# Two graph layers on one core: the second layer's denominators move into the pass that computes its scores, and TensorE's counts in the edge passes are raised by drains

## What is computed

```python
# layer one: attention with 8 heads of 32, over the edges of each destination
score = clip(sum(q[dst] * k[src]) / sqrt(32), -10, 10)
alpha = softmax over the edges of one dst
wv = segment_sum(alpha * v[src], dst);  y = wv @ Wp.T + bp;  x1 = x + y
x1 = x1 + gelu(layernorm(x1) @ W1.T + b1) @ W2.T + b2
x = layernorm(x + x1)
# layer two: scores per edge, softmax over the edges of one SOURCE
z = leaky_relu(proj_s[src] + proj_t[dst], 0.2)
e = z @ W_attn.T
e_exp = exp(e - max of e over the edges of src)
denom = segment_sum(e_exp, src)
agg = segment_sum(x[src] * (e_exp / denom[src]), dst)
x = layernorm(x + agg @ W_fc.T + b_fc)
```

## Time and profile before

| what | us |
|---|---|
| median of three runs | 3942.93 |
| lowest and highest of them | 3939.38, 3952.08 |
| span of the profiled execution | 3995.8 |
| PE, PEld busy in it | 2303.1, 1677.2 |
| DVE, ACT, POOL busy in it | 2175.4, 1124.8, 1960.5 |

### The profile page before, as it was taken

How to read it: one execution, slowest core, us unless ns; L and a number is a source line. 1 busy time by engine, 2 the same in 40 slices (tenths; PEclk the granted TensorE clock), 3 DMA queues, 4 the chain that set the end, 5 groups by cost and what they waited for, 6 DMA issues and landing times.

```text
span 3995.8 us, 54572 instructions
## 1 busy us (share of the span) xinstructions
PE 2303.1 (58%) x11454; PEld 1677.2 (42%) x11455; DVE 2175.4 (54%) x6197; ACT 1124.8 (28%) x2699; POOL 1960.5 (49%) x1970
## 2 busy tenths in 40 slices
PE   4456666666666664878233333333334395777776
PEld 2244444444444443756122222222122294656655
DVE  5455655556555564242344444444444596677676
ACT  0144554445544553333111111111112100111111
POOL 0255555555555553121566666666656303544443
PEclk9788877788778877988666666667666656988898
DMA  4666656666666663121677777777767505666564
GB/s 141 195 179 178 182 176 180 175 180 181 177 178 176 176 177 100 50 86 47 191 215 221 212 211 214 211 214 228 210 206 216 175 0 186 205 197 204 183 208 150
DMA packets 365707, 698.62 MB, mean 175 GB/s; under 512 B 77317, under 2 KB 247039, under 8 KB 365674
## 3 DMA queue, kind: packets, MB, share of 16 engines
q0 software_dynamic: 134784, 425.63, 36.1%
q1 hardware_dynamic: 220602, 256.40, 20.6%
q10 hardware_dynamic: 10288, 16.23, 1.1%
HBM read 597.23 MB, written 100.85 MB: 175 GB/s over the span
## 4 chain that ended last, share of the span: by engine, by line
another core or an unknown queue 27%; PE 26%; DVE 24%; issue 16%; DMA 3%; DVEq 2%; SPq 1%; POOL 1%; ACT 1%; ACTq 0%; POOLq 0%
PE ps_px L900 7%; DVE sb_prod L1622 4%; DVE sb_wide L1615 4%; DVE sb_score L1468 4%; PE ps_pa L913 3%; PE ps_px L913 2%; PE ps_px L998 2%; PE ps_px L1007 2%; PE ps_pa L1058 2%; PE ps_pn L1045 2%; DVE sb_wide L1477 1%; PE ps_px L876 1%; DVE sb_parts L1814 1%; DVE sb_prod L1462 1%
## 5 line engine op out<-in xcount | busy, mean ns | idle before, releaser
L900 PE MATMUL ps_px<-sb_parts 128*128 x2430 | 468.2, 358 | 798.8 <-DVE sb_wide L1615 563.1
L900 PEld LDWEIGHTS ps_px<-sb_parts 128*128 128x128 bf16 x2430 | 268.1, 122 | 999.4 <-DVE sb_wide L1615 625.6
L779 POOL DMA_INDIRECT sb_ring<-kv_rows,sb_idx x324 | 322.5, 995 | 357.8 <-DVE sb_wide L1477 152.6
L913 PE MATMUL ps_pa<-sb_wide,sb_onehot 128*128 128x264 f32 x864 | 302.8, 483 | 317.1 <-DVE sb_wide L1477 256.2
L779 POOL DMA_INDIRECT sb_ring<-proj_rows,sb_idx x324 | 316.5, 977 | 303.8 <-issue 170.8
L779 POOL DMA_INDIRECT sb_parts<-kv_rows,sb_idx x324 | 316.0, 975 | 206.9 <-DVE sb_wide L1477 107.4
L1142 ACT ACTIVATE sb_parts<-sb_bits,sb_nn_tab 128x768 bf16<-128x768 int16 x135 | 126.3, 937 | 1016.6 <-remote 606.9
L900 PE MATMUL ps_px<-sb_parts,sb_xwm 128*128 x2430 | 397.9, 309 | 19.2 <-ACT sb_xwm L1147 14.6
L779 POOL DMA_INDIRECT sb_w<-narrow_rows,sb_idx x324 | 315.3, 973 | 163.7 <-issue 102.2
L913 PE MATMUL ps_px<-sb_wide,sb_onehot 128*128 128x264 f32 x756 | 252.9, 466 | 197.3 <-DVE sb_wide L1477 124.3
L779 POOL DMA_INDIRECT sb_w<-feat_rows,sb_idx x162 | 158.9, 981 | 416.0 <-issue 192.3
(11 more groups left out here) (256 smaller groups left out, 4473.2 us busy)
## 6 DMA issues: line engine op xcount, KB each, us to landing
sb_bits<-dst_short SPq DMA_DIRECT2D x280, 192.0 KB
x_edges<-sb_ring SPq DMA_DIRECT2D x54, 768.0 KB
sb_slots<-x_edges SPq DMA_DIRECT2D x54, 768.0 KB
x_edges<-sb_slots SPq DMA_DIRECT2D x27, 768.0 KB
sb_w<-x_edges SPq DMA_DIRECT2D x27, 768.0 KB
sb_msg<-lo_rows SPq DMA_DIRECT2D x28, 576.0 KB
kv_rows<-sb_slots ACTq DMA_DIRECT2D x25, 256.0 KB, 2.8
sb_parts<-part_rows SPq DMA_DIRECT2D x28, 193.5 KB
```

The source lines that it names most:

```text
L779: pool.indirect_dma_start(out=out[:, i, :], out_offset=None, in_=rows, in_offset=bass.IndirectOffsetOnAxis(ap=idx[:, 2 * p + i:2 * p + i + ...
L900: mm = pe.matmul(into, hots_t[L][:, 2 * p + i, :], flat(visit_parts[:, bass.ds(parity, 1), a, 0:width]), start=(a == 0), stop=(a == 2))
L913: mm = pe.matmul(into[:, 0:C + H], onehot[:, j, :], sums_in[:, 2 * (p % FLIGHT) + i, :], start=(p % EARLY == 0 and i == 0), stop=True, ski ...
```

## The change

**Denominators.** They are summed in pass two: the visit v's while pass two is at v + 1. ACT takes the exponentials of the visit's 30 columns, and makes the one-hots of the sources' low bits, 30 rows and 5 Relus, behind the next visit's destination one-hots. DVE does the split and the product in small steps between the pairs 3 to 7; PE does the 30 matmuls in five sets of six behind `expand` of the pairs 10 to 14. As shift it takes the maximum over the first visit, found by a transpose and a matmul on PE during the second. The last visit's share comes after the loop. The slow path gets a sum of its own. `x1` is read in five parts, each waited for by its part of `feats`, and pass three's first one-hots are built ahead of `feats`.

**Counts.** In pass one `expd[0]` and `summed` become one semaphore, `stepped`, raised by a drain once a step, after both `sum_pair(p)` and `expand(p + 9)`. In pass two a drain behind each `expand` raises `expd[1]`, and one behind each set of denominators raises `dpe`. In pass three a drain behind each `sum_rows` raises `slots_free[2]`. A drain is an instruction of its own behind the matmuls, which carries the count in their place.

```diff
@@ expand
-                        mm = pe.matmul(into, hots_t[L][:, 2 * p + i, :], flat(visit_parts[:, bass.ds(parity, 1), a, 0:width]),
-                                       start=(a == 0), stop=(a == 2))
-                mm.then_inc(expd[L], 1)
+                        pe.matmul(into, hots_t[L][:, 2 * p + i, :], flat(visit_parts[:, bass.ds(parity, 1), a, 0:width]),
+                                  start=(a == 0), stop=(a == 2))
+                if L:
+                    pe.drain().then_inc(expd[1], 1)
@@ sum_pair
-                mm.then_inc(summed, 1)
@@ pass one, PE's visits
                         expand(0, C, after, v + 1, p + AHEAD - PAIRS)
+                    pe.drain().then_inc(stepped, 1)
@@ pass two, PE
-            with pe.Fori(0, TD // DT // 2) as it:
-                for b in range(2):
-                    pe.wait_ge(dv, it * 2 + b + 1)
-                    for j in range(DT):
-                        mm = pe.matmul(pn[:, 0:3 * W], lo_hot[:, b, :, j], hi_ex[:, b, :, :, j].rearrange("p a n -> p (a n)"),
-                                       start=False, stop=True, skip_group_check=True)
-                    mm.then_inc(dpe, 1)
+            def denominators(v, g):
+                if g == 0:
+                    pe.wait_ge(dv, v + 1)
+                pe.wait_ge(den_lo, v * HALVES + g + 1)
+                for j in range(g * R, (g + 1) * R):
+                    pe.matmul(pn[:, 0:3 * W], lo_hot[:, j, :], hi_ex[:, :, :, j].rearrange("p a n -> p (a n)"),
+                              start=False, stop=True, skip_group_check=True)
+                pe.drain().then_inc(dpe, 1)
...
+                for p in range(PAIRS):
+                    expand(1, CW, parity, v, p)
+                    if second and p == 2:
+                        top_transposed()
+                    if second and p == 4:
+                        top_spread()
+                    if earlier is not None and p >= PAIRS - HALVES:
+                        denominators(earlier, p - (PAIRS - HALVES))
@@ pass three, sum_rows
-                mm.then_inc(slots_free[2], 1)
+                pe.drain().then_inc(slots_free[2], 1)
@@ ACT, pass two
+            def score_exps(v):
+                act.wait_ge(zs, v * len(ZS) + ZS["masked"])
+                act.wait_ge(shift_set, 3)
+                act.activation(ex_v, dots[:, 2], ACT.Exp, bias=shift[:, 0:1]).then_inc(den_ex, 1)
+
+            def low_sources(v):
+                t0 = visit_value(act, "tile", v)
+                for g in range(HALVES):
+                    act.wait_ge(dpe, v * HALVES + g + 1)
+                    act.sem_inc(act_seen, 1)
+                    for j in range(g * R, (g + 1) * R):
+                        ins = act.activation(lo_hot[:, j, :], iota[:], ACT.Abs, bias=src_lo[:, bass.ds(t0 + j, 1)], scale=-1.0)
+                    ins.then_inc(lo_away, 1)
...
+            node_half(0)
+            with act.Fori(0, total - 1) as u:
+                node_half(act.snap(u + 1))
+                score_exps(u)
+                low_sources(u)
+            low_sources(last_visit(act))
+            score_exps(last_visit(act))
@@ DVE, pass two
+                if step == "high":
+                    t0 = visit_value(dve, "tile", v)
+                    dve.tensor_tensor(hi_hot, iota_j, src_hib[:, bass.ds(t0, G)].unsqueeze(1).broadcast_to([P, W, G]), ALU.is_equal).then_inc(dh, 1)
+                if step == "ex":
+                    dve.wait_ge(den_ex, v + 1)
+                    dve.tensor_tensor(left0, ex_v, kept, ALU.mult).then_inc(dsplit, 1)
...
+                if step == "spread":
+                    done("part2")
+                    dve.wait_ge(dh, v + 1)
+                    dve.wait_ge(dpe, v * HALVES + HALVES)
+                    dve.tensor_tensor(hi_ex, hi_hot.unsqueeze(1).broadcast_to([P, 3, W, G]),
+                                      ex_parts.unsqueeze(2).broadcast_to([P, 3, W, G]), ALU.mult).then_inc(dv, 1)
+
+            WEIGHED = {3: ["ex"], 4: ["part0"], 5: ["left1"], 6: ["part1", "high"], 7: ["left2", "part2", "spread"]}
@@ waits on PE's counts, pass one
-                dve.wait_ge(expd[0], v * PAIRS + p + 1 + PAIRS)
+                dve.wait_ge(stepped, v * PAIRS + p + 1 + PAIRS)
...
-                act.wait_ge(summed, v * PAIRS + p + 1)
+                act.wait_ge(stepped, v * PAIRS + p + 1 + AHEAD + PAIRS - FLIGHT)
@@ SP, after pass two
-            sp.dma_start(x1, proj_rows[:, CW:ROW].rearrange("(w p) c -> p w c", p=P)).then_inc(x1_back, 16)
+            for i in range(NB):
+                some = slice(i * W // NB, (i + 1) * W // NB)
+                sp.dma_start(x1[:, some], proj_rows[i * W // NB * P:(i + 1) * W // NB * P, CW:ROW].rearrange("(w p) c -> p w c", p=P)).then_inc(x1_back[i], 16)
...
-            sp.wait_ge(fv, FVS["recip2"])
             low_rows(tile)
+            features(0)
+            sp.wait_ge(fv, FVS["den0"])
             for c in range(THIRDS):
                 stream(tile, c)
-            features(0)
```

More of the change, by code:

```diff
@@ L289, in build @@
         hot = [sem(f"hot{L}") for L in (0, 1)]
-        expd = [sem(f"expd{L}") for L in range(2)]
+        expd = [None, sem("expd1")]
         dgs = sem("dgs")
@@ new lines, in _, with scored, rows, attend @@
+            WEIGHED = {3: ["ex"], 4: ["part0"], 5: ["left1"], 6: ["part1", "high"], 7: ["left2", "part2", "spread"]}
+            def scored(v, earlier=None, second=False):
+                t0 = visit_value(dve, "tile", v)
+                def rows(p):
+                    dve.wait_ge(expd[1], v * PAIRS + p + 1 + PAIRS)
+                    landed(dve, 1, total, v, p)
+                    dve.tensor_tensor(zbuf[:, pair(p), :], px[:, places(p), 0:CW], proj_slots(p)[:, :, 0:CW], ALU.add).then_inc(slots_free[1], 1)
+                def attend(p):
+                    dve.wait_ge(slots_free[1], v * PAIRS + p + 1 + PAIRS)
+                    dve.tensor_copy(low_dots[:, :, 2 * p:2 * p + 2].rearrange("p c j -> p j c"), zbuf[:, pair(p), C:CW])
+                    for i in (0, 1):
+                        ins = dve.scalar_tensor_tensor(out=prod[:, p % 3, i * C:i * C + C], in0=zbuf[:, 2 * (p % FLIGHT) + i, 0:C], scalar=0.0, in1=attn_hi[:],
+                                                       op0=ALU.max, op1=ALU.mult, accum_out=dots[:, 0, 2 * p + i:2 * p + i + 1])
+                    if p == PAIRS - 1:
+                        ins.then_inc(zs, 1)
+                rows(0)
+                for p in range(PAIRS):
+                    if p + 1 < PAIRS:
+                        rows(p + 1)
+                    attend(p)
+                    if second and p == 0:
+                        dve.wait_ge(shift_pe, 1)
+                        dve.tensor_reduce(top[0:1, 1:2], pa[0:1, 0:P], AX, ALU.max).then_inc(shift_set, 1)
+                    if second and p == 2:
+                        dve.wait_ge(shift_pe, 2)
+                        dve.tensor_scalar(shift[:], pa[:, P:P + 1], -1.0, None, ALU.mult).then_inc(shift_set, 1)
+                    if earlier is not None:
+                        for step in WEIGHED.get(p, []):
+                            weighed(earlier, step)
+                def at(name):
+                    return v * len(ZS) + ZS[name]
+                dve.wait_ge(zs, at("dots"))
+                dve.tensor_tensor(dots[:, 1], dots[:, 0], low_dots[:, 0], ALU.add).then_inc(zs, 1)
+                dve.wait_ge(zs, at("low"))
+                dve.tensor_tensor(dots[:, 2], dots[:, 1], low_dots[:, 1], ALU.mult).then_inc(zs, 1)
+                dve.tensor_copy(kept, low_dots[:, 1]).then_inc(zs, 1)
+                dve.wait_ge(zs, at("kept"))
+                if earlier is None:
+                    dve.tensor_reduce(top[:, 0:1], dots[:, 2], AX, ALU.max).then_inc(shift_set, 1)
+                some = e_all[:, bass.ds(t0, G)]
+                dve.tensor_tensor(some, some, dots[:, 2], ALU.add).then_inc(zs, 1)
+                dve.wait_ge(zs, at("added"))
+                dve.sem_inc(dve_seen, 1)
@@ L1643, in _ @@
+            scored(0)
+            scored(1, 0, second=True)
+            with dve.Fori(0, total - 2) as u:
+                scored(dve.snap(u + 2), dve.snap(u + 1))
             for c in range(THIRDS):
@@ L1645, in _ @@
                 dve.sem_inc(dve_seen, 1)
+            last = last_visit(dve)
+            for step in ("high", "ex", "part0", "left1", "part1", "left2", "part2", "spread"):
+                weighed(last, step)
             dve.memset(e_all[:, T:TPAD], -FAR).then_inc(sv, 1)
@@ L1837, in _ @@
             high_onehots(0)
+            for i in range(NB):
+                some = slice(i * W // NB, (i + 1) * W // NB)
+                dve.wait_ge(x1_back[i], 16)
+                dve.tensor_tensor(feats[:, some, :], x1[:, some, :], denom[:, 2, some].unsqueeze(2).broadcast_to([P, W // NB, C]), ALU.mult).then_inc(fv, 1)
             reciprocals(0)
```

194 lines of the change are left out of this document (107 added, 87 removed).

## The result

The changed kernel took 4121.53 us (median of four runs, 4112.31 to 4139.45) against 3947.51 for the kernel before on the same chip (median of four, the three shown ahead and one more): a ratio of 1.0453, 95% interval 1.042 to 1.0486. It is slower by 4.5%, where 3430 us was forecast. The profiled execution has a span of 4117.1 us, 121.3 more than that of the kernel before, 3995.8.

What follows compares the result with a forecast made beforehand. Bound taken as POOL's gather issue plus waits for late matmul-carried counts. Pass one -265, pass two -122, pass three -12, tail -121 sum to -520: 3995.8 to 3476, scaled to 3430 us; range 3330 to 3560, 8 in 10 3330 to 3870.

Steps and rivals of the forecast that it cites:

- What bounds the kernel: Passes one and two: POOL's gather issue is the floor, 37.7 us a visit; above it, matmul-carried counts arrive 6 to 19 late.
- The old stage, -121: Between last scores and pass three's first gather: moving denominators into pass two saves 121 us, bounds -130 to -108.
- What pass two takes on: Pass two: moved denominator work on DVE, PE and ACT hides under POOL's 37.7 us a visit; 3.3 left for it and other waits.
- The drains, 0.45 where PE is the bound: All three passes: each drain costs 0.45 us where PE is the bound, 0 where it waits anyway; bounds 0.05 and 1.2.
- -554: Whole kernel: sum in us if a drain cost only 0.18 us, pass three's exposed drains costing 24 instead of 60.
- a third, 60 us: Pass three: the share taken of its drains' full 182 us, since PE idles 6.0 of 24.0 us a visit.
- The late counts: All passes: drain counts arrive promptly, so late-count waits go; passes one and two fall to 41 us a visit, pass three -12.
- -265 and -122: Forecast savings in us from passes one and two, each falling to 41 us a visit from 51.2 and 45.7.
- Rival A: All passes: drains wait for late completions and stop PE; at 1.2 us a drain +191, 4130 us scaled; chance 0.15.
- B: All passes: a drain's count is as late as a matmul's, nothing cured; 3883 us scaled; chance 0.08.
- C: Passes one and two: partial cure, pass one falls to 46 us a visit, pass two gains nothing; 3679 us scaled; chance 0.12.
- D: Pass two: DVE's new bf16 steps hold up POOL's issue, at most 2 us a visit, +52 us, inside the forecast's range.

Runs made afterwards that it cites:

- drains_p1: Kernel before with only pass one's two counts merged into one raised by a drain, chip 0: ratio 1.022, pass one 1395.2 us.
- change_third: The changed kernel run again, against the kernel before on chip 12, which has no late counts: ratio 1.0115.
- no_gathers_p1_b: drains_p1 with pass one's gathers after the first visit replaced by POOL writing one column, late chip 11, one run: pass one 873.3 us.
- p3_bare: Kernel before with a drain carrying nothing behind each pass-three sum_rows, count still on the matmul, chip 15: ratio 1.0439, pass three 598.8 us.
- p3_twice: Kernel before with two drains behind each pass-three sum_rows, the second carrying the count, chip 15: ratio 1.0554, pass three 633.7 us.

## Why the prediction was wrong

*What bounds the kernel.* Right in what it saw, as far as it went: POOL's issue is the floor, and on the chips without late counts passes one and two lie on it at 39 us. But the trace was taken for the kernel's own nature. It was also the chip's.

*The old stage, -121.* Right: 133.3 to 13.8 is -119.5, the first gather 4 us sooner, together -124.

*What pass two takes on, nothing beyond a share of 3.3 a visit.* On the chips without late counts 15 us, 0.6 a visit: right. On the late chips 22 to 51 us: 0.9 to 2 a visit, inside the share that was left, but of a gain that did not come.

*The drains, 0.45 where PE is the bound.* Right: 0.45 to 0.55 measured between two groups in a row (1.32 to 1.42 for 0.87), 0.34 in the mean of pass three; the loss of overlap and the restart were both there. The Trainium skill's 175 ns alone (TensorE: Matmul & The Clock Gate, Single matmul latency) would have been too little: the 0.20 of idle comes on top. (The sum that the prediction gives for it, -554, should be -556: 24 for 60 in -520.) The term mis-sized was how many drains bind in pass three. I took a third, 60 us, for PE's idle 6.0 us a visit; without late counts they cost 137 us, as if three in four bound at 0.45, and on the late chips +99 to +118 went with them. PE's idle time absorbed little of them.

*The late counts.* This is the step that failed: "If a drain's count arrives when PE is empty, the waits above lose their cause." It does arrive when PE is empty, but PE isn't empty, for a drain, until the held completions are in. What the trace showed at 2612.86 and 2626.90 was a late completion and not a slow message: a drain in the same place is as late, and PE's next group with it. (The update of the count behind 2626.90 is itself recorded at 2626.87, for a matmul that ends at 2607.85. Since PE's ends are modelled, the records can't tell whether the matmul ends late or only its acknowledgement.) A drain inherits the lateness and adds PE's stop: before, PE went on with up to nine pairs while a count hung; with drains it stands (the earlier trace rows against 2199.13 and 2208.29 above). -265 and -122 were forecast for passes one and two; the drains alone measured +65 to +73 and +25 to +33 on chip 0.

*Rival A* was this mechanism, at 4130 us near the 4121.5 measured, with 0.15. Its sum came close by luck. It had passes one and two unchanged, pass three +312 at an even 1.2 us a drain and, through it, +191; measured are +37, +77 and +106. The price isn't even: most drains cost 0 or 0.34 us, more than one in four of passes one and two 3 to 4 us (the mean of 116 and of 105). The Trainium skill's PSUM — Partial Sum Buffer, Engine vs sequencer instructions, had the rule that held: the increment on the matmul, a drain for a barrier. And the evidence offered against the rival, the drain at the end of the program, ran without gathers, where nothing is late.

*Its chance* was too low for the evidence. The rows showed lateness only beside gathers and no drain beside any, so they could not tell a late message from a late completion; I put 0.60 on the one and 0.15 on the other.

*Rivals B, C and D.* Not B: its counts stay late, as they did, but by it pass one would have kept its length. Not C: pass one did not gain. D stays small on the chips without late counts: all the moved work costs 15 us there.

## What to carry to other kernels

A drain in place of a count on a matmul brought no completion sooner in any of these runs; it stops PE, for 0.34 us in the mean of pass three and 0.45 to 0.55 between groups in a row, and it waits out whatever holds the completion back. When counts arrive late, ask first whether the completion or the message is late. One run beforehand tells: leave the count on the matmul, put a drain that carries nothing behind it, and read how long after the last matmul the drain ends. And where a trace shows waits with no releaser, run the kernel on a second chip before a change is built on them.

## What the runs showed of the hardware

- On the chip of the record and two of the five behind it (3947 to 4014 us for the kernel before) PE's completions were held back while indirect gathers were in issue or in transfer, up to 15 us; on the other three (3274 to 3276 us) no drain was late. What differs between the chips no run shows, nor whether recording has a part in it: on the late chips 16 to 40% of the semaphore updates that instructions make in a pass with gathers have no record, on the others 1% at most, in every trace of this case.
- Without gathers, pass one takes 870 to 873 us on either kind, PE's granted clock 1.00 (the full 2.4 GHz), for 0.83 with them in drains_p1 on a late chip: on the late chips gathers cost pass one over 450 us, on the others some 150.
- SP is slowed in the same stretches: from 2100 to 2600 us, in pass two, gaps of 0.6 to 0.8 us between the starts of two of its instructions fill 37% of the time in the kernel before and 2% in change_third; in no_gathers_p1_b they fill 2% of 500 to 1000 us, in pass one without gathers, and 36% of 2100 to 2600. DVE's and ACT's counts of passes one and two showed no such lateness where they have a record: in the kernel before the updates by L1462, L1477, L1615 and L1161 stand some 0.01 us behind the end of the instruction, none over 0.3 us behind.
- A drain behind each pair of pass three costs 0.45 to 0.55 us between groups in a row, 0.20 to 0.30 of it idle, and 0.34 in the mean of all 405 (p3_bare); a second one right behind it 0.09 (p3_twice).
